# Attention block with two mixing layers: key norms moved into the products, value tiles emptied in pairs, query factors as whole rows, and another order of the steps

## The reference, cut to what matters

```python
# first layer, 8 heads of 128
f_q, f_k, f_v = (proj(q), proj(k), proj(v))          # layer_norm @ w_in.T, split by head
dots = einsum('hqnd,hqmd->hqnm', f_q, f_k)
cosine_sim = dots / (qn[..., :, None] * kn[..., None, :])   # norms of queries and keys
q_ratio = 2.0 * minimum(q_var, 1.0) / (q_var + 1.0)         # k_ratio likewise
var_component = einsum('hqn,hqm->hqnm', q_ratio, k_ratio)
mixed = cw * cosine_sim + vw * cov_component + ww * var_component
out = einsum('hqnm,hqmd->hqnd', mixed, f_v)          # then @ w_out.T + b_out
# second layer, 16 heads of 16: softmax of scores, times values,
# @ Wo, l2 norm, @ Wff, l2 norm, gelu; each layer is gated and added to x
```

## Time and profile before

| | |
|---|---|
| time, median of 3 runs | 1545.91 us (1535.48 to 1546.38) |
| the profiled execution | 1539.16 us |
| its span from the first to the last instruction | 1537.4 us |
| PE busy | 1308.2 us, 85% |
| DVE busy | 1155.9 us, 75% |
| ACT busy | 1019.8 us, 66% |
| granted TensorE clock | 0.963 of 2.4 GHz, mean |

### The profile page before, as it was taken

How to read it: one execution, slowest core, us unless ns; L and a number is a source line. 1 busy time by engine, 2 the same in 40 slices (tenths; PEclk the granted TensorE clock), 3 DMA queues, 4 the chain that set the end, 5 groups by cost and what they waited for, 6 DMA issues and landing times.

```text
span 1537.4 us, 35793 instructions
## 1 busy us (share of the span) xinstructions
PE 1308.2 (85%) x10706; PEld 868.5 (56%) x10706; DVE 1155.9 (75%) x3191; ACT 1019.8 (66%) x3381; POOL 199.5 (13%) x129
## 2 busy tenths in 40 slices
PE   5988756889898989898989898989898989898855
PEld 2655635465656565656565565656565656574622
DVE  5878465577877887878787787878787969696845
ACT  5564112276777777777777777768686868685767
POOL 2441031000101010101010101010101010101000
PEclk9999868999999999999999999999999999999978
DMA  8420002261616160716160807161616162626160
GB/s 255 139 91 17 3 10 63 53 107 40 134 38 134 33 138 28 138 33 137 34 131 13 148 24 144 28 138 34 126 46 115 56 111 61 111 61 111 49 110 15
DMA packets 182906, 125.05 MB, mean 81 GB/s; under 512 B 16430, under 2 KB 180431, under 8 KB 182800
## 3 DMA queue, kind: packets, MB, share of 16 engines
q1 hardware_dynamic: 182800, 124.00, 37.1%
HBM read 87.00 MB, written 25.77 MB: 73 GB/s over the span
## 4 chain that ended last, share of the span: by engine, by line
PE 32%; SPq 18%; DVE 12%; issue 12%; DMA 7%; ACT 3%; DVEq 0%; POOL 0%; POOLq 0%; ACTq 0%
PE work L861 9%; PE work L863 9%; PE work L862 9%; SPq L1178 7%; SPq L1169 5%; DMA sqE<-sq_rows 4%; SPq L1205 3%; DVE nm L1624 3%; PE attended L1346 2%; ACT prob L1435 2%; DMA qstack<-parts 2%; PE score L1334 2%; PE work L1241 1%; DVE l2s L1594 1%; DMA parts<-kl 1%
## 5 line engine op out<-in xcount | busy, mean ns | idle before, releaser
L1435 ACT ACTIVATE prob<-score,nm 128x256 f32<-128x256 f32 x1024 | 484.3, 514 | 30.9 <-DVE nm L1624 28.8
L1624 DVE TENSOR_REDUCE nm<-score 128x2 f32<-128x512 f32 x512 | 339.1, 682 | 36.8 <-PE score L1334 34.2
L1334 PE MATMUL score<-qstack,kstack 128*128 128x256 f16 x1024 | 193.8, 280 | 92.4 <-ACT prob L1435 45.9
L1435 ACT ACTIVATION_READ_ACCUMULATOR prob<-score,nm 128x1 f32 x1024 | 252.5, 247 | 0.0
L1334 PEld LDWEIGHTS score<-qstack,kstack 128*128 128x128 f16 x1024 | 80.0, 99 | 177.3 <-ACT prob L1435 111.1
L1550 DVE BATCH_NORM_STATS2 qst<-work 128x6 f32<-128x128 f32 x512 | 112.4, 284 | 68.7 <-PE work L863 68.7
L1346 PE MATMUL attended<-prob,vsp 128*32 128x256 f32 x2048 | 135.7, 388 | 1.4 <-DVE vsp L1638 1.4
L861 PE MATMUL work<-woutTh,fvph 128*128 128x256 f16 x384 | 105.8, 275 | 13.4 <-ACT v L1420 13.1
L1481 POOL TENSOR_TENSOR rq<-qft,mhalf 128x32 f32<-128x32 f32 x16 | 86.8, 5428 | 226.6 <-DVEq L1558 226.6
L861 PE MATMUL work<-xTh,Gh 128*128 128x256 f16 (+1 forms) x320 | 89.5, 280 | 28.3 <-DVE md L1580 28.3
L862 PE MATMUL work<-woutTl,fvph 128*128 128x256 f16 x384 | 105.5, 275 | 0.0
(11 more groups left out here) (327 smaller groups left out, 3288.9 us busy)
## 6 DMA issues: line engine op xcount, KB each, us to landing
kstack<-parts SPq DMA_DIRECT2D x256, 64.0 KB, 4.0
qstack<-parts SPq DMA_DIRECT2D x256, 64.0 KB, 4.2
sqE<-sq_rows SPq DMA_DIRECT2D x64, 154.0 KB
s_xin<-in_x SPq DMA_DIRECT2D x8, 1024.0 KB, 6.0
xin<-in_x SPq DMA_DIRECT2D x16, 512.0 KB, 3.4
x2S<-in_x SPq DMA_DIRECT2D x16, 512.0 KB, 4.7
x<-x2S SPq DMA_DIRECT2D x16, 512.0 KB, 4.1
out<-zb SPq DMA_DIRECT2D x16, 512.0 KB, 5.2
```

The lines of the kernel that those rows point to most:

```text
L1334: last = nc.tensor.matmul(sc[n % SC][:, jj * NQ:(jj + 1) * NQ], kstack[:, e, j, b2 * NQ + k * P:b2 * NQ + (k + 1) * P], qstack[:, j, b2 * ...
L1435: nc.scalar.activation(prob[:, g % PG, k, u % 4, :], sc[n % SC][:, jj * NQ:(jj + 1) * NQ], ACT.Exp, bias=nm[:, u:u + 1], accum_out=sums[:, ...
L1624: nc.vector.tensor_reduce(nm[:, 2 * n:2 * n + 2], sc[n % SC][:, :].rearrange("p (u q) -> p u q", q=NQ), AX.X, ALU.max, negate=True).then_i ...
```

## The change

- Key norms: `V` is emptied without `rkc`, and as one operation for both tiles of a bank. The factor goes into `d0.o` to `d5.o`, which becomes one operation for each tile (product times `rkc` times `sqE`) where it was one for each bank. The constants that `rk_all` is scaled with follow.
- Query factors: `aux` shrinks to two quarters of 32 columns. `a0` becomes two steps of four transposes: `a1` (ratios, `wqT`) and `a0` (cosine factors, `sqT`), each giving 8 rows of 512. `sq_rows` is 8 rows of 2 KB and is stored and loaded by whole rows; the `wqT` copies are 2 DMAs in a step `wq` of their own.
- VectorE program: a copy in `moments` goes, `rs` is written over `sums`, and waits that an earlier wait of the same engine implies are left out, on other engines too.
- There are 47 names with a bank now, and `ORDER` is another list.

```diff
@@ the emptying of V, and the products d
+        if kind == "V":
+            b2, tiles = c // 3, HM_TILES[c % 3]
+            r, n = HM_ROWS[tiles[0]], len(tiles)
+            return (Vp[half][0:r, b2, tiles[0]:tiles[-1] + 1, :],
+                    bk[0:r, 0:n * DIM].rearrange("p (t o) -> p t o", o=DIM), 1.0 / WS)
...
-                    for dst, src, scale, hi in value_tiles(e, "l"):
-                        last = nc.vector.scalar_tensor_tensor(dst, src, scale, hi, ALU.mult, ALU.subtract)
...
-                    dve.wait_ge(sq_in, a * SQ_LOADS * 16 + SQ_LOADS * 16)
+                    if c == 0:
+                        dve.wait_ge(rkc_ready, a + 1)
+                        dve.wait_ge(sq_in, a * SQ_LOADS * 16 + SQ_LOADS * 16)
...
-                    drain(nc.vector.tensor_tensor(
-                        md[0:r, c % 2, 0:n * 2 * P].rearrange("p (t n) -> p t n", n=2 * P),
-                        bank(e)[0:r, 0:n * 2 * P].rearrange("p (t n) -> p t n", n=2 * P),
-                        sqE[0:r, tiles[0]:tiles[-1] + 1, b2 * NQ:(b2 + 1) * NQ], ALU.mult), e)
+                    for m, t in enumerate(tiles):
+                        last = nc.vector.scalar_tensor_tensor(
+                            md[0:r, c % 2, m * 2 * P:(m + 1) * 2 * P], bank(e)[0:r, m * 2 * P:(m + 1) * 2 * P],
+                            rkc[0:r, t, b2:b2 + 1], sqE[0:r, t, b2 * NQ:(b2 + 1) * NQ], ALU.mult, ALU.mult)
+                    drain(last, e)
@@ the query factors on PE, ACT and SP
-                    pe.wait_ge(wqr_ready, a + 1)
-                    pe.wait_ge(sq_ready, a + 1)
-                    last = nc.tensor.transpose(bk[:, 0:P], aux[:].rearrange("p s t h -> p (s t h)"), ident[:])
+                    pe.wait_ge((sq_ready, wqr_ready)[c], a + 1)
+                    for t in range(PT):
+                        last = nc.tensor.transpose(bk[0:H, t * P:(t + 1) * P], aux[:, c, t, :], ident[:])
...
+                    drain(nc.scalar.activation(sqT[:], bank(e)[0:H, :], ACT.Copy), e)
...
-                    sp.dma_start(sq_rows.rearrange("t h n -> (t h) n"), sqT[:]).then_inc(sq_stored, 16)
+                    sp_wait(sq_in, a * SQ_LOADS * 16)
+                    sp.dma_start(sq_rows, sqT[:]).then_inc(sq_stored, 16)
+                elif step == "wq":
+
+                    sp_wait_drained(a, "a1")
+                    sp_wait_filled(a - 1, "y1")
                     for half in "hl":
-                        for t in range(PT):
-                            sp.dma_start(mT[half][KR_ROW:KR_ROW + H, t // 2, HT - 1, t % 2 * P:(t % 2 + 1) * P],
-                                         wqT[half][(PT + t) * H:(PT + t + 1) * H, :]).then_inc(wq_in, 16)
+                        sp.dma_start(mT[half][KR_ROW:KR_ROW + H, :, HT - 1, :],
+                                     wqT[half][:].rearrange("h (b n) -> h b n", b=2)).then_inc(wq_in, 16)
...
-                            sp.dma_start(sqE[lo:hi, t, :].rearrange("p (t n) -> p t n", n=P),
-                                         sq_rows[:, h, :].partition_broadcast(hi - lo)).then_inc(sq_in, 16)
+                            sp.dma_start(sqE[lo:hi, t, :], sq_rows[h, :].partition_broadcast(hi - lo)).then_inc(sq_in, 16)
@@ moments, and the first lines of ORDER
-    link(k0 + 4, nc.vector.tensor_copy(ft[:, 5, :, :], ft[:, 1, :, :]))
...
-rk qs1 V0 qpow S0 G0 V0.h M0 S1 S2 G0.h G1 M1 X0 V0.l X1 G0.l S3 G2 M2 G1.h S4 M3 V1 G2.h X2 G1.l G2.l X3 qs2 S5 M4 a0
+rk V0 qs1 G0 V0.h S0 qpow V1 G0.h M0 V0.l X0 G0.l S1 V1.h a1 M1 S2 S3 a1.h M2 G1 X1 V1.l G1.h M3 V2 ldr X2 a1.l S4
+V2.h qs2 S5 G1.l X3 a0 V2.l G2 M4 G3 a0.v M5 G2.h S6 aux X4 V3 R0 M6 G3.h G2.l X5 S7 P0 M7 V3.h G3.l G4 X6 sqe V3.l S8
```

More of the change, by code:

```diff
@@ L913 @@
 SC_CREDIT = SCORES
-A_STEPS, B_STEPS = 12, GROUPS + 5
+A_STEPS, B_STEPS = 11, GROUPS + 5
 ORDER = """
-rk qs1 V0 qpow S0 G0 V0.h M0 S1 S2 G0.h G1 M1 X0 V0.l X1 G0.l S3 G2 M2 G1.h S4 M3 V1 G2.h X2 G1.l G2.l X3 qs2 S5 M4 a0
[L924 to L932, removed]
+rk V0 qs1 G0 V0.h S0 qpow V1 G0.h M0 V0.l X0 G0.l S1 V1.h a1 M1 S2 S3 a1.h M2 G1 X1 V1.l G1.h M3 V2 ldr X2 a1.l S4
+V2.h qs2 S5 G1.l X3 a0 V2.l G2 M4 G3 a0.v M5 G2.h S6 aux X4 V3 R0 M6 G3.h G2.l X5 S7 P0 M7 V3.h G3.l G4 X6 sqe V3.l S8
+G5 G4.h M8 S9 X7 V4 G4.l M9 X8 R1 S10 X9 S11 M10 P1 G5.h X10 G5.l S12 V5 M11 ldy V4.h M12 S13 wq d0 X11 V4.l ldx V5.h
+M13 S14 X12 d1 V5.l R2 X13 M14 S15 P2 d0.o X14 M15 S16 m0.h d1.o fk0 M16 m0.l S17 fk0.h d2 E0 fk0.l d3 X15 M17 m1.h
+d2.o S18 X16 d4 m1.l M18 X17 R3 S19 d5 m2.h M19 X18 S20 m2.l P3 d3.o X19 d4.o fk1 m3.h M20 m3.l X20 S21 S22 z y0 m4.h
+fk1.h d5.o L0 m5.h M21 E1 R4 X21 M22 zT0 S23 m4.l X22 P4 fk1.l zT0.h m5.l S24 y0.o S25 y1 zT0.f M23 L1 X23 M24 M25 X24
+R5 X25 zT0.l zT1 y1.o O0 zT1.h ln1 S26 O0. S27 P5 zT1.f M26 lpow O1 M27 X26 ln2 X27 S28 S29 M28 O1. zz0 zz1 zT1.l
+zz0.h S30 R6 fk2 zz1.h zz0.l X28 P6 zz1.l fk2.h M29 S31 pk0 M30 X29 M31 X30 fk2.l pk1 X31 pq0 pk0.h R7 pk1.h pk0.l P7
+E2 pq0.h pk1.l L2 pq1 pq0.l E3 L3 O2 pq1.h pq1.l O3 O2. parts q0 O3. q1 F1 q0.o pv0 q1.o back0 F2 q2 pv0.v q3 q2.o F3
+q4 q3.o q5 q4.o q6 q5.o F4 q7 q6.o res pv1 back1 q7.o pv1.v out
 """.split()
@@ L1275, in a_part @@
                     if c == 0:
-                        wait_drained(pe, a, *(f"G{g}" for g in range(6)))
+                        wait_drained(pe, a, "G5")
                     for n, t in enumerate(tiles):
@@ L1383, in a_part @@
                         drain(ins, e)
-                elif e[0] == "V" and part == "h":
-                    wait_filled(act, a, e)
-                    act.wait_ge(rkc_ready, a + 1)
-                    for dst, src, scale, _ in value_tiles(e, "h"):
-                        last = nc.scalar.activation(dst, src, ACT.Copy, scale=scale)
-                    last.then_inc(hi_ready[lead(e)], 1)
-                elif e == "a0" and part == "h":
+                elif e == "a0" and part == "v":
                     wait_filled(act, a, e)
                     act.wait_ge(sq_stored, a * 16)
-                    act.wait_ge(wq_in, a * 128)
-                    nc.scalar.activation(sqT[:], bank(e)[0:PT * H, 0:P], ACT.Copy)
-                    nc.scalar.activation(wqT["h"][PT * H:2 * PT * H, :], bank(e)[PT * H:2 * PT * H, 0:P], ACT.Copy,
-                                         scale=MS).then_inc(hi_ready[lead(e)], 1)
+                    drain(nc.scalar.activation(sqT[:], bank(e)[0:H, :], ACT.Copy), e)
+                elif e == "a1" and part == "h":
+                    wait_filled(act, a, e)
+                    act.wait_ge(wq_in, a * 32)
+                    nc.scalar.activation(wqT["h"][:], bank(e)[0:H, :], ACT.Copy, scale=MS).then_inc(hi_ready[lead(e)], 1)
                 elif part == "h":
@@ L1475, in a_part @@
                     pool.wait_ge(rk_kept, 2)
-                    wait_drained(pool, a - 1, *(f"V{n}" for n in range(6)))
+                    wait_drained(pool, a - 1, "d5")
                     nc.gpsimd.tensor_copy(rkc[:, 0:HT - 1, :], rk_all[:, 0:HT - 1, bass.ds(2 * a, 2)])
@@ L1488, in b_part @@
                 if step == "F1":
-                    wait_drained(pool, b, *(f"O{n}" for n in range(PT)))
+                    wait_drained(pool, b, f"O{PT - 1}")
                     nc.gpsimd.tensor_tensor(nrs[:].rearrange("p j t -> p (j t)"), nrm[:].rearrange("p j t -> p (j t)"),
```

85 lines of the change are left out of this document (37 added, 48 removed).

## The result

The changed kernel takes **1459.8 us** (median of 4 runs, 1458.1 to 1463.4) against 1541.2 for the kernel before in the same comparison (1535.5 to 1546.4): ratio 0.948, 95% interval 0.943 to 0.952. It is 81 us faster. The profiled execution took 1463.4 us, its span is 1461.7, the granted clock 0.967.

The account below looks back on a forecast made before the run. No single engine bounds: PE's work is the floor, its idle time comes from late chains over other engines. Turn 38.6 + 33.9 + 3.0 + 0.6 = 76.1 against 77.2; 1.1 counted 15 times, 16 us off 1539.2, gives 1523, range 1494 to 1556.

Parts of the forecast that it names:

- The 3.8 I keep: DVE's unexplained idle time ahead of qs1, at the loop's jump back: assumed to stay 3.8 us a turn.
- if the 3.8 at the jump changes: Stated sign of being wrong: DVE's 3.8 us of nothing ahead of qs1 comes out different.
- The end of the turn: DVE from q7.o to M0: 7.3 us instead of 8.6, M0 1.3 earlier; net gain at this place 1.0 a turn.
- The wait at `a1`: PE, meeting a1 early, waits some 2.5 us there for the end of qs1 and V0 emptied; its longest wait.
- The chain of `sqE`: Store, then loads: DVE gets sqE 38.6 us after parts, bounds 35 and 42, wants it at 37.0, waits 1.6.
- the rule of engines: A DMA splits over the largest number up to 16 dividing its slowest dimension; loads would stay near 11.3, turn 1.9 longer.
- After `sqE`: DVE from sqE to the next parts: 33.9 us of work, 3.0 of waits and 0.6, together 37.5.
- Values and products: On DVE: V.l falls from 3.9 to 3.2 us a turn, d.o rises by the same 0.7; no gain.
- The base: Turn of the kernel before, from one parts to the next on SP, read as 77.2 us.
- The short chain: Rival: sqE is there at 35, before DVE asks at 37.0; turn 74.5, 40 us less, 1499; chance 0.15.
- The slow rival: d0 asks too early: store 4.2, loads 11.3, sqE at 41.7; turn 79.2, 30 us slower, 1569; chance 0.18.
- The change doesn't do what it says: Rival: the 3.8 at the jump grows, M0 no earlier, time about 1539; chance 0.27 together with PE absorbing the gain.

Follow-up runs that it names:

- e1: Kernel before with only the VectorE shortening (copy in the moments and implied waits left out), old order and old forms: 1509.6 us, ratio 0.979.
- e2: Kernel before with 64 tiny VectorE memsets run once ahead of the loop, nothing taken out: 1525.0 us, ratio 0.991.
- e3: Changed kernel with 16 tiny VectorE memsets ahead of its main phase, outside the loop: 1494.9 us, ratio 0.971.
- e4: Changed kernel with 20 long satisfied waits added inside VectorE's loop, ten instructions more in the body: 1517.2 us, ratio 0.984.
- e7: Changed kernel with the old forms of V and d (key norm multiplied in where V is emptied, one d.o operation per bank): 1452.9 us, ratio 0.944.
- e12: Changed kernel with x2S and xin loads and both wqT copies issued ahead of the sqE loads in SP's queue: 1491.4 us, ratio 0.968.
- e11: e1's kernel with SP issuing the xin load, then the sqE loads, behind the sq_rows store, ahead of the wqT copies: 1453.8 us, ratio 0.944.

## Why the prediction was wrong

**The step that failed** is "The 3.8 I keep: it stands at the jump back of the loop." The change made DVE's program 5 instructions shorter ahead of the loop and 10 shorter in it, and the gap went to nothing. e1 and e2 take it away in the old kernel, by trimming and by moving; e3 and e4 put it back in the new one, by moving and by lengthening. The prediction named this as a sign of being wrong ("if the 3.8 at the jump changes"), but gave it no term in that direction. In all fourteen kernels the gap and some 65 more packets of instructions come together. They come at the same time too: in the kernel before, one packet of the instruction queue falls into the gap of the earlier trace rows (699.06 to 702.82 us), and so it is in 12 of its 13 gaps. What decides fits blocks of 256 instructions: with one offset of 181 to 195 for instructions that my count leaves out, the loop bodies at 525 to 843, 536 to 844 and 530 to 848 touch three blocks and have the gap; those at 518 to 822, 520 to 828 and 589 to 907 touch two and have none, nor have the other eight, which lie between 518 and 828. The Trainium skill ("Runtime: NRT & Kernel Launch", section "Instruction fetch mechanics") says that the engine's instruction memory holds 32 KiB, two pages of 256 instructions, and that a branch back to a page outside these has to fetch it first; the rows agree in that the gap and the packets come and go with the place of the body. They don't show why it is five packets of some 8 KB a turn; three pages would be six of them, an estimate from the 16 KiB that this section of the Trainium skill gives a page. The offset is fitted and not seen, and that DVE stands still until the packet is there is inferred from the times.

**What the gap costs** depends on what stands behind it. In the new kernel it costs about its own length: 33.7 us of gap and 35.1 us of time in e3, 58.1 and 57.4 in e4. In the old one the gap adds up to 50.4 us, and e2, without it, is only 15 us faster (1.0 a turn). Other waits take its place there: from 400 to 1350 us 47.5 us of gap go, DVE's waits for scores rise from 4.7 to 34.2 us and the one for `sqE` from 18.6 to 24.6. So the 3.8 that the prediction kept would have cost the new kernel 13 x 3.8 = 49 us, an estimate from e3 and e4; the forecast missed by 63.

The terms in the order of the forecast, in us a turn:

- *The end of the turn.* Forecast 7.3 from `q7.o` to `M0`, measured 3.7: the difference of 3.6 is the gap, the rest of it was right. The wait at `a1` was to be 2.5 and PE's longest; there is none, since it hung on the gap too (e3, with the gap, has 1.9: 22.2 in 12). What PE waits there is the 0.55 ahead of `V2`.
- *The chain of `sqE`.* Forecast: data on DVE 38.6 after `parts`; measured 36.7. The store goes out at 23.6 (forecast 26.2, the gap again), has landed at 25.3 at the latest (1.7, I had 3.0), and from the first load to use it is 11.4 (I had 9.4; the bound of 11.3, 732.85 - 721.43 = 11.4 when worked out again, was what the rule of engines gave). Two errors of size against each other, -1.3 and +2.0. DVE would have wanted the data at 35.4, forecast 37.0, and waits 1.3 in this turn, 1.7 in the mean. The wait of 1.6 was forecast, for partly wrong reasons.
- *After `sqE`.* Forecast 37.5 to the next `parts`, measured 36.9 (769.18 to 806.08). Right. Along this path the turn comes out: 76.1 - 2.6 (the gap) - 1.3 + 2.0 - 0.6 = 73.6. So but for the gap the sum held, in part because the two errors of size nearly cancel, which is luck.
- *Values and products.* Taken as no gain. e7 differs by 0.6 a turn, 7 us, less than can be told from no change.
- *The order.* Costed along this one path. It put `sqE` 7.0 earlier (45.6 to 38.6) and gave 5.9 of that back to the work that stands behind it now (37.5, where it was 764.46 - 732.85 = 31.6). e12 shows what the place of the loads in SP's queue is worth in the new kernel (31.6 us) and e11 against e1 in the old (55.8 us).
- *The base.* I took the one turn that I had read, 77.2, for the mean, which is 78.3.

In the profiled times, the forecast's 1523.2 and the measured 1463.4 are 59.8 apart: 14 x (76.1 - 73.83) = 32 in the turns, 14 x (78.31 - 77.2) = 16 in the base, and 12 ahead of the second `parts` that had no term (5.1 us are won before the first `parts`, 7.6 between the first and the second). The gap isn't in that last part: its first time is at 386 us, behind the second `parts`, and e3, which has the gap, has its second `parts` as early as the changed kernel (361.0 us against 361.7). What it is stays open.

**The rivals.** The short chain came nearest (turn 74.5, 1499), with the wrong reason: its `sqE` was to be there before DVE asks. The slow rival had the loads right (11.3) and was refuted by the store, which lands in 1.7 behind `out`, and by the gap. "The change doesn't do what it says ... because the 3.8 at the jump grows" had the right place and the wrong sign: a gap that the profile calls "issue" and that I could not explain should have carried a chance of going, too, and by the earlier trace rows that was 3.76 x 13 = 49 us, more than all the other terms together.

**What is left of the 81 us.** The parts don't add up, since each is priced with the others in place: with a gap of 33.7 us back in its place 35 less, with the loads late in the queue 32 less, without whole rows 22 less, in the old order 57 less, with the old forms of `V` and `d` 7 more.
